# Edge phase of a three-layer graph network: the mask of a pair of tiles split in two and placed between the next pair's transposes

## The reference

```python
Q = (h @ Wq.T + bq).reshape(-1, H, DH)     # H = 4, DH = 64
K = (h @ Wk.T + bk).reshape(-1, H, DH)
V = (h @ Wv.T + bv).reshape(-1, H, DH)
scores = jnp.einsum('ehd,egd->ehg', Q[src], K[tgt]) / jnp.sqrt(jnp.float32(DH))
attn = jax.nn.softmax(scores, axis=-1)
msg = jnp.einsum('ehg,egd->ehd', attn, V[tgt]).reshape(-1, HID)
msg = msg + Ee[et]
proj = msg @ Wo.T + bo
return jax.ops.segment_sum(proj, src, num_segments=n_nodes)
```

## Time and profile before

| what | value |
|---|---|
| time, median of 3 runs | 3674.46 us |
| runs | 3674.46, 3678.60, 3667.35 us |
| the profiled execution, its span | 3674.3 us (no own time is listed beside the span) |
| PE, PEld busy | 3426.8 us (93%), 2968.4 us (81%) |
| DVE, ACT, POOL busy | 2458.4 us (67%), 2698.7 us (73%), 2459.9 us (67%) |
| granted PE clock, mean | 0.974 |

### The profile page before, as it was taken

The page is one execution under the profiler, slowest core; times in us unless marked ns, Lnnn a source line. Parts: engine busy times, 40 slices in busy tenths (PEclk is TensorE's granted clock), DMA queues, the critical chain, the costliest instruction groups (busy, mean ns, idle before and its releaser), DMA issues.

```text
span 3674.3 us, 87831 instructions
## 1 busy us (share of the span) xinstructions
PE 3426.8 (93%) x25408; PEld 2968.4 (81%) x25409; DVE 2458.4 (67%) x6794; ACT 2698.7 (73%) x8426; POOL 2459.9 (67%) x2552
## 2 busy tenths in 40 slices
PE   6888879999999998999999999899999998969998
PEld 2444559999999966999999986799999997759998
DVE  7888447777777765777777775577777777931111
ACT  4999678888888856888888876788888885424443
POOL 3777127777777775777777776677777776725443
PEclk9999879999999999999999999999999999979999
DMA  2000257777777726777777753677777776446664
GB/s 80 1 1 1 90 207 205 208 208 207 207 208 206 206 94 193 205 208 207 207 206 207 208 160 115 206 206 206 209 206 207 206 207 195 155 155 182 185 176 120
DMA packets 264903, 630.75 MB, mean 172 GB/s; under 512 B 56095, under 2 KB 128726, under 8 KB 256471
## 3 DMA queue, kind: packets, MB, share of 16 engines
q0 software_dynamic: 161376, 477.59, 46.5%
q1 hardware_dynamic: 103431, 152.05, 12.4%
HBM read 577.72 MB, written 52.04 MB: 171 GB/s over the span
## 4 chain that ended last, share of the span: by engine, by line
PE 47%; POOL 18%; issue 17%; DMA 10%; DVE 5%; ACT 2%; DVEq 0%; POOLq 0%; SPq 0%; ACTq 0%
POOL arena L573 12%; PE bank L1570 10%; DMA arena<-kv_d,gidx 9%; PE bank L1560 8%; POOL rec_d L557 6%; PE bank L1761 5%; PE bank L1545 5%; PE bank L1773 5%; PE bank L1529 4%; PE bank L1523 2%; PE bank L1553 2%; PE bank L1605 2%; PE bank L1611 1%; DVE att L857 1%; PE bank L1683 1%
## 5 line engine op out<-in xcount | busy, mean ns | idle before, releaser
L573 POOL DMA_INDIRECT arena<-kv_d,gidx x1764 | 1763.6, 1000 | 729.1 <-issue 529.8
L1570 PE MATMUL bank<-att,arena 128*128 128x128 f32 x7056 | 946.3, 278 | 22.9 <-DVE att L857 19.4
L1560 PEld LDWEIGHTS bank<-qbd,kt_s 128*128 128x128 f32 x7056 | 932.2, 193 | 33.2
L1560 PE MATMUL bank<-qbd,kt_s 128*128 128x128 f32 x7056 | 934.8, 276 | 0.0
L1570 PEld LDWEIGHTS bank<-att,arena 128*128 128x128 f32 x7056 | 862.4, 193 | 42.0 <-DVE att L857 39.9
L828 DVE TENSOR_REDUCE sc<-bank 128x32 f32<-128x512 f32 x882 | 607.6, 689 | 313.7 <-PE bank L1560 301.7
L1306 ACT ACTIVATE kt_s<-bank 128x512 f32<-128x512 f32 x882 | 526.6, 597 | 253.3 <-PE bank L1545 239.8
L1545 PE MATMUL bank<-ident,arena 128*128 128x128 f32 x3528 | 623.4, 283 | 61.7 <-DMA arena<-kv_d,gidx 49.4
L857 DVE TENSOR_TENSOR att<-at_s,oh 128x512 f32<-128x512 f32 x882 | 608.3, 690 | 25.9
L1545 PEld LDWEIGHTS bank<-ident,arena 128*128 128x128 f32 x3528 | 407.9, 142 | 163.9 <-DMA arena<-kv_d,gidx 124.2
L875 DVE TENSOR_TENSOR arena<-stage,arena 128x64 f32 x1764 | 398.2, 226 | 196.1 <-DVE arena L875 112.4
(11 more groups left out here) (246 smaller groups left out, 3999.8 us busy)
## 6 DMA issues: line engine op xcount, KB each, us to landing
arena<-in_pack SPq DMA_DIRECT2D x56, 1030.0 KB, 5.1
arena<-kv_d,gidx POOLq DMA_INDIRECT x1764, 3.7
oh<-oh_d SPq DMA_DIRECT2D x222, 64.0 KB
kv_d<-arena SPq DMA_DIRECT2D x50, 256.0 KB, 2.0
xin<-hid_d SPq DMA_DIRECT2D x75, 128.0 KB, 2.2
arena<-in_w SPq DMA_DIRECT2D x8, 1024.0 KB, 7.2
kv_d<-arena SPq DMA_DIRECT2D x5, 1280.0 KB, 5.1
hid_d<-arena SPq DMA_DIRECT2D x50, 128.0 KB, 2.0
```

Source lines behind the costliest of these rows:

```text
L573: pool.indirect_dma_start(kv[:, t // UB, t % UB, :], None, kv_d, bass.IndirectOffsetOnAxis(gidx[:, h, t - h * HT:t - h * HT + 1], 0),).the ...
L1560: ins = mm(bk[:, o:o + P], kt_s[:, p % 2, u, c, :], qbd[:, p % 4, u, :], start=False, stop=(c == KC - 1), skip_group_check=True)
L1570: ins = mm(bank[5 + p % 3][:, o:o + P], kv[:, b, u, D + g * DH:D + (g + 2) * DH], att[:, b % 2, u, :, g:g + 2, :].rearrange("p s g h -> p ...
```

## The change

In the edge phase of PE alone. The mask of pair p is now two matmuls of 256 columns, one for each tile of the pair, each with the same weights (oh) as before. The first has the start flag; both write to the same bank. They stand in keys_masks, behind the first and behind the second transpose of the next pair's first tile. The second tile's two transposes follow without a mask. The wait for score_read, and once in four pairs that for oh_landed, have moved with the mask ahead of the transposes, where keys had no wait except gathered. In the last step of a layer, where there is no next pair, the two halves stand alone ahead of the aggregation. Nothing changes on the other engines.

```diff
             def e_phase(l):
-                def keys(p, landed):
-                    for t in (2 * p, 2 * p + 1):
-                        pe.wait_ge(gathered[t], landed)
+                def key(p, u, c):
+                    t = 2 * p + u
+                    o = u * D + c * P
+                    return pe.transpose(bank[3 + p % 2][:, o:o + P], kv[:, t // UB, t % UB, c * P:(c + 1) * P], ident[:, :])
+
+                def mask(p, u):
+                    m = 2 * (p % 4) + u
+                    mm(bank[p % 3][:, u * D:(u + 1) * D], oh[:, p // 4, 1, :],
+                       maskc[:, m:m + 1, :].to_broadcast([P, H, DH]),
+                       start=(u == 0), stop=False, skip_group_check=True)
+
+                def keys_masks(k, landed, p, at, here):
+                    if p is not None:
+                        pe.wait_ge(S.score_read, at[p + 1])
+                        if p % 4 == 0:
+                            pe.wait_ge(oh_landed[p // 4], here[p // 4 // 2])
+                    for u in range(2):
+                        if k is not None:
+                            pe.wait_ge(gathered[2 * k + u], landed)
                         for c in range(KC):
-                            o = (t % 2) * D + c * P
-                            ins = pe.transpose(bank[3 + p % 2][:, o:o + P], kv[:, t // UB, t % UB, c * P:(c + 1) * P], ident[:, :])
-                    ins.then_inc(S.kT_done, 1)
+                            if k is not None:
+                                ins = key(k, u, c)
+                            if u == 0 and p is not None:
+                                mask(p, c)
+                    if k is not None:
+                        ins.then_inc(S.kT_done, 1)
 
-                def scores(p, at, here):
+                def scores(p, at):
                     bk = bank[p % 3]
-                    pe.wait_ge(S.score_read, at[p + 1])
-                    if p % 4 == 0:
-                        pe.wait_ge(oh_landed[p // 4], here[p // 4 // 2])
-                    mm(bk[:, :], oh[:, p // 4, 1, :],
-                       maskc[:, 2 * (p % 4):2 * (p % 4) + 2, :].unsqueeze(2).to_broadcast([P, 2, H, DH]),
-                       start=True, stop=False, skip_group_check=True)
                     pe.wait_ge(S.kT_ready, at[p])
...
                     for p in range(pairs):
                         if p + 1 < pairs:
-                            keys(p + 1, here[(p + 1) * 2 // PAIRS])
+                            keys_masks(p + 1, here[(p + 1) * 2 // PAIRS], p, at, here)
                         elif not last:
-                            keys(0, ahead)
+                            keys_masks(0, ahead, p, at, here)
+                        else:
+                            keys_masks(None, None, p, at, here)
                         if p >= LAG or not first:
                             aggregate((p - LAG) % PAIRS, at[p])
-                        scores(p, at, here)
+                        scores(p, at)
```

More of the change, by code:

```diff
@@ L1581, in turn @@
                         if p + 1 < pairs:
-                            keys(p + 1, here[(p + 1) * 2 // PAIRS])
+                            keys_masks(p + 1, here[(p + 1) * 2 // PAIRS], p, at, here)
                         elif not last:
-                            keys(0, ahead)
+                            keys_masks(0, ahead, p, at, here)
+                        else:
+                            keys_masks(None, None, p, at, here)
                         if p >= LAG or not first:
                             aggregate((p - LAG) % PAIRS, at[p])
-                        scores(p, at, here)
-                keys(0, pe.snap((l * NTURN + 1) * 16))
+                        scores(p, at)
+                keys_masks(0, pe.snap((l * NTURN + 1) * 16), None, None, None)
                 turn(0, True, False)
```

## The result

The changed kernel takes 3721.8 us in the median of 4 runs, the kernel before, beside it, 3671.2: a ratio of 1.0135 [1.012, 1.0149]. I had forecast 3674 with 3638 to 3711. It is slower, and outside the range; it lies on the figure of rival A, 3722.

A forecast was written before the change was run, and what follows sets the result against it. POOL's gathers were taken to bound the kernel, 2.61 us a pair against PE's 2.44. The span of 3674.3 less 0.7 at layer ends, plus 0 for held gathers, gave 3673.6, stated as 3674 us, range 3638 to 3711.

The forecast's parts named there:

- rival A: Gathers that now start just before L857 fall under it and are held more: slower, 3722 us; chance 0.23.
- POOL sets the pace: In the edge phases POOL's gathers take 2.61 us a pair, PE needs 2.44, and POOL never waits for PE.
- Steps 1, 3, 4: Mask split costs 0; waits moved ahead of the transposes cost 0; aggregation up to 0.22 us later gains nothing.
- Step 5: At each layer's end one mask no longer stands between aggregation and scores: 0.22 us in 3 layers, 0.7 us gained.
- Step 2: Mask fills PE's stop for the second tile: PE saves nothing, but scores end 0.22 us sooner after the landing.
- Step 6: Gathers held by L857, which comes up to 0.22 us earlier: 48 us either way possible, taken as 0.
- C: PE becomes the bound because the mask halves expose their weight loads: 273 us slower, 3947; chance 3%.
- D: PE is the bound after all and the mask in the stop counts: up to 150 us faster, 3524; chance 2%.

The follow-up runs named there:

- tenth run: Kernel before plus one more matmul of 256 columns, overwritten by the mask, in front of the mask: 3668.6 against 3672.8 us, ratio 0.9986.
- first run: Kernel before with the mask split in two halves at its old place behind the aggregation: 3673.3 against 3674.0 us, ratio 1.000.
- eighth: Changed kernel with both mask halves back in front of the scores, only the earlier waits kept: 3671.9 against 3673.1 us for the kernel before.
- third: Changed kernel with the mask halves behind the second tile's transposes instead of the first's: 3719.6 us, ratio 1.0127 to the kernel before.
- sixteenth run: Kernel before with the whole, unsplit mask moved ahead of the aggregation, behind all four transposes: 3716.9 us, ratio 1.0108.
- fifth run: Kernel before with L857's product replaced by a reduction with one SBUF input, leaving out the one-hot matrix: 3588.1 us, ratio 0.9772.
- fourth run: Changed kernel with only one mask half moved, the other in front of the scores: 3740.1 us, ratio 1.0178 to the kernel before.
- thirteenth run: Changed kernel with an idle DVE reduction ahead of L828 for the third L857 behind a softmax: 3722.4 us, ratio 1.0115 to the kernel before.
- fifteenth: Changed kernel with an idle DVE reduction ahead of L828 for the second and third L857 behind a softmax: 3641.7 us, 0.991 to the kernel before.
- fourteenth: Kernel before with an idle DVE reduction ahead of L828 for the second L857 behind a softmax: 3652.5 us, ratio 0.9935.
- eleventh run: Kernel before with L857 in four instructions of 128 elements: 3663.9 us, ratio 0.9978.

## Why the prediction was wrong

- **POOL sets the pace: right.** The three windows grew by 49 us where the gathers grew by 48, and PE took 97 us of added work for nothing (tenth run).
- **Steps 1, 3, 4: right.** The split costs 0 (first run), the moved waits cost 0 (eighth), POOL never waits for the aggregation beyond its 0.30 us. By the sentence of the Trainium skill weighed in step 1 (TensorE: Matmul & The Clock Gate, Part 3, The mechanism) the second weight load would have stood on PE's path; the halves follow at 0.11 us and the trace still does not agree with it. Step 5's 0.7 us is less than these runs can tell.
- **Step 2: half right.** The stop is filled and gives PE nothing. But "the scores end 0.22 us sooner after the landing" is not what acts. With the scores as late behind the landing as before, the third and the sixteenth run are nearly as slow (1.0127 and 1.0108). At the place shown PE is released by L857, and what counts is that the mask left the stretch between aggregation and scores.
- **Step 6: the step that failed.** "So the present distances are no better or worse than chance, and a shift has no reason to gain or lose ... I take 0." The measured value is +48.0 us of longer gathers, beside 46.2 us more of span. The sum over all distances, 85 by chance and 95 measured, hid that they are not independent: L857 comes 1.73 us after L857 while DVE has a backlog and a held gather 1.72 us after a held one, so that one hold brings the next. One of the four rows quoted had its gather at 0.08 us, the distance that repeats, and I took it for one value among others. For the third L857 the change meant crossing the start of a gather, from 0.11 behind it to 0.08 ahead, and that is 0.48 us at once. I had read such a crossing off the rows (962.29, "some 0.4 more"), and yet priced a shift with the 0.22 of a gather that was and stays held.
- **The range.** Rival A had the mechanism, gathers held more. I cut the range at three quarters of its 48 us, with no row behind that cut. That its 3722 us was also the size is luck: the 48 stood on 0.22 us more for one spread in four, and the traces have 0.29 and 0.21 us more at two places of twelve, less at two and up to 0.11 more at the others. What it cites of the Trainium skill (SBUF — State Buffer, Who interferes with whom) fits the fifth run for the gathers: with one SBUF input they are free. For the other direction the trace does not agree: 658 L857 of the kernel before start inside a gather, and they take 0.68 us on average and 0.72 at most.
- **C and D** did not come about: POOL's idle time ahead of the gathers stayed (729.8 against 729.1 us), and the windows grew.

Not settled is the total. The time follows the mean of L573 (+60 us of gathers and +66 of time in the fourth run, -88 and -85 in the fifth). Which pairs are held in a steady state, and so why half the move costs more than all of it, stays open. I take it to be the outcome of a loop: holds delay gathers, these land later and move PE and DVE. The thirteenth run, in which a hold is removed in one pair and others grow, fits this. I can say of one pair, with less than half of the added holds, how the change tipped it; I cannot compute the sum.

## What to carry to other kernels

If POOL's queue of indirect DMAs sets the pace, read the spread of one DMA's duration before anything else, and look which DVE instruction with two SBUF inputs runs at the start of the long ones: to cut it in two was worth 1.2% here, and without its second input (and without the product) the kernel was 2.3% faster. Where two engines step at nearly the same period, a move that costs and frees nothing can tip them into lockstep; such an effect has no sign that could be read from an average, so the range must hold both outer values. Added work on an engine that does not set the pace was free as work (tenth and fifteenth runs). What it does to the distances is another matter: against the kernel before, the same 0.2 us on DVE came with 0.6% and 0.9% less in the fourteenth and fifteenth run, and with 1.2% more in the thirteenth, where the change alone had cost 1.35%.

## What the runs showed of the hardware

- A gather that starts while L857 runs, a DVE instruction of 0.68 us with two SBUF inputs, takes 1.42 us in place of 0.95 at 0.08 us behind its start, less the later it starts, and nothing more from 0.55 us on (kernel before). One that started 0.06 us ahead of L857 is not held (0.94), and L857 is not slowed by starting inside a gather: 658 of them take 684 ns on average, 719 at most.
- A matmul of 256 bf16 columns with its own load of weights takes 0.11 us of the stream between two f32 transposes of 128, at 2.4 GHz granted (clock 1.00 there).
- Small DVE instructions have a price of their own: L857 of 512 elements takes 0.69 us, one of four with 128 elements 0.29 us, 1.15 for all four by their durations, which overlap somewhat; it made PE wait (eleventh run).
